# Third group of pair sums moved to the PSUM bank of the first, parts of layer 2 moved two banks on, one gather moved on GpSimd's queue

## The chip, the cores and the metric

The kernel runs on one core of one Trainium2 chip. The metric is the device time of one execution in microseconds (us). TensorE is called PE in the profile, VectorE DVE, ScalarE ACT, GpSimd POOL and SyncE SP. The time of the kernel before is 2491.37 us, the median of 3 runs (2491.12 to 2492.53).

## What is computed

48 embedding tables are looked up for 512 samples, which gives `e` with 48 fields of 32 elements a sample. Three layers of a compressed interaction network follow, each with 128 outputs, and then three dense layers:

```python
def _cin_layer(xi, x0, W, b):
    Wr = W.reshape(Fi, F0, -1)
    out = jnp.einsum('nie,nje,ijo->noe', xi, x0, Wr) + b[None, :, None]
    return jax.nn.relu(out)
x0 = e
xs = [x0]
for W, b in ((W1, b1), (W2, b2), (W3, b3)):
    xs.append(_cin_layer(xs[-1], x0, W, b))
z = jnp.concatenate(xs, axis=1).sum(axis=-1)
h = jnp.concatenate([z, dense_ctx], axis=1)
h = jnp.maximum(h @ W_top1 + b_top1, 0.0)
h = jnp.maximum(h @ W_top2 + b_top2, 0.0)
y = h @ W_top3
```

## The kernel before

**Tiles.** A tile is 128 samples at one of the 32 elements, so there are 4 blocks of 32, 128 tiles in all. Each goes through three layers, and the engines work as a software pipeline: step `v` does the pair sums of layer 1 for tile `v+3` (t0), the products of layer 1 for tile `v+2` (t1), layer 2 for `v+1` (t2) and layer 3 for `v` (t3). In the code `l` is 0 for what leads from layer 1 to layer 2 and 1 for what leads from layer 2 to layer 3. Each of the five engines has its own list of instructions, written out by hand, and they meet at semaphores alone.

**Layer 1** uses that its input is symmetric: products of two fields come out of squares of sums. The fields of the tile, split in a high and a low half-precision part, stand in `x0hl`; a transposing DMA issued by SP (`transpose_x0`, L263) brings them to `x0T`; `pair_sums` (L439) multiplies them with a 0/1 matrix in three groups of 4, 4 and 2 matmuls of 128 columns (groups 0, 1 and 2, ahead of banks 12, 14 and 17 of the step); `square_pairs` on ACT (L589 to L594) squares each group out of PSUM, twice; `stacked_lo` on DVE (L757) makes the low part of the last group, `squares_lo` on POOL (L356) that of the others; and `layer1` (L456) multiplies them with the weights in 28 matmuls of 128 columns, spread over banks 1 to 5 of the next step, into `misc[0]`.

**Layers 2 and 3** have 12 banks each a tile (bank numbers 0 to 11 of a step are layer 2, 12 to 23 layer 3). PE fills a PSUM bank with 3 matmuls of 512 columns (L466), in a ring of 5 banks. ACT and DVE take turns in emptying them, with 4 instructions a bank: ACT writes scaled products (L564), DVE adds into two chains (`fma`, L778). POOL adds up ACT's products (`sum_rest` L332, `sum_all` L345 to L351), helped by one adding DMA of 512 KB a layer and tile, `work<-work` (`add_by_dma`, L325).

**From one layer to the next.** DVE merges the parts (L787, L792), ACT takes the relu (L601), DVE works out a scale in four small steps (L807 to L819), ACT writes the high part (`hi_part`, L608) and the scaled columns (L612), DVE the low part (`lo_part`, L824). Behind the low part SP issues two transposing DMAs, `xT<-hi` and `xT<-lo` (L270, L271). The program of SP in a step is `transpose_x(1, t3)`, `transpose_x0(t0)`, `transpose_x(0, t1)`, in this order, each behind waits of its own. In step `v` the high and low part of `l = 1` stand at bank 1 (ACT) and bank 3 (DVE), those of `l = 0` at banks 8 and 9. DVE's instructions of a bank come only once PE has filled this bank.

**POOL's queue** in a step: `sum_all(1, t3-1)`, `add_by_dma(0, t2)`, every second step `x0_scaled`, two gathers (indirect DMAs, L293, in 24 of the steps of each of the first three blocks), every second step `x0_lo`, then `sum_rest(0)`, `sum_all(0)`, `add_by_dma(1, t3)`, `squares_lo`, and `sum_rest(1)`.

Of the kernel before, what the change touches and what calls it, by code (L numbers as in the profile page):

```python
# [33 lines left out]
P = 128  # L34
# [29 lines left out]
KF = KT - 1  # L64
L1_PASSES = 3 * KF + 1
SETUP = W1_SETUP + 2 * BANKS
PAIR_BANK = (1, 0, 0)
PAIRS_AT = (12, 14, 17)
LAST_USER = [max(m for m in range(BANKS) if (BANKS + m) % RING == r) for r in range(RING)]
SCALE = 4  # L70
# [8 lines left out]
def build(nc, ids, tables, ctx_in, select, pairs_of, w_pair, w_pair_t, w2, w3, b_cin, wt1, bt1, wt2, bt2, wt3, out):  # L79
# [3 lines left out]
    with ExitStack() as stack:  # L83
# [9 lines left out]
        def wait(eng, s, value):  # L93

            if not (isinstance(value, int) and value <= 0):
                eng.wait_ge(s, value)  # L96
# [15 lines left out]
        wst, zst = w1h[:, KF, :], sb("zst", [P, P], f16)  # L112
# [51 lines left out]
        misc = [ps(f"m{n}", [P, Q * P]) for n in range(2)]  # L164
# [23 lines left out]
        s_zt, s_zts = sem("pair_sums_in_psum"), sem("squares_saved")  # L188
        s_zst, s_zl = sem("stacked_squares_ready"), sem("squares_lo")
# [38 lines left out]
        def active(tile):  # L228

            return not isinstance(tile, int) or 0 <= tile < TILES  # L230
# [59 lines left out]
        def _(pool):  # L290
            def gather(b, fields, landed=None):
                for f in fields:
                    pool.indirect_dma_start(  # L293
                        emb[:, b, f, :], None, tables[f],
                        bass.IndirectOffsetOnAxis(ap=ids_sb[:, b, f:f + 1], axis=0)).then_inc(landed or s_gather[b], 16)
# [57 lines left out]
            def squares_lo(t):  # L353

                wait(pool, s_zts, t * 3 + 3)
                pool.tensor_tensor(zl[:], zT[:, 0:KF, :], zh[:], ALU.subtract).then_inc(s_zl, 1)  # L356
# [12 lines left out]
            def step(v, parity, b=None, fields=(), columns=None):  # L369

                t0, t2, t3 = v + 3, v + 1, v
                if active(t3 - 1):
                    sum_all(1, t3 - 1)
                if active(t2):
                    add_by_dma(0, t2)
                if parity == 0 and active(v + 4):
                    x0_scaled(v + 4)
                gather(b, fields)
                if parity == 0 and active(v + 4):
                    x0_lo(v + 4)  # L380
                if active(t2):
                    sum_rest(0, t2)
                    sum_all(0, t2)
                if active(t3):
                    add_by_dma(1, t3)
                if active(t0):
                    squares_lo(t0)
                if columns:
                    spread(b, *columns)
                if active(t3):  # L390
                    sum_rest(1, t3)
# [19 lines left out]
        def _(pe):  # L411
# [17 lines left out]
            def pair_sums(t, g):  # L429

                if g == 0:
                    wait(pe, s_x0t, (t + 1) * 16)
                    wait(pe, s_zts, (t - 1) * 3 + 1)
                elif g == 1:
                    wait(pe, s_pool[0], t + 1)
                else:
                    wait(pe, s_zts, t * 3 + 2)
                for k in range(4 * g, min(4 * g + 4, KT)):
                    ins = nc.tensor.matmul(misc[PAIR_BANK[g]][:, (k % 4) * P:(k % 4 + 1) * P],  # L439
                                           sel[:, k * P:(k + 1) * P], x0T[0:2 * F, :], start=True, stop=True)  # L440
                ins.then_inc(s_zt, 1)
# [4 lines left out]
            def layer1(t, c):  # L446

                if c == 0:
                    wait(pe, s_zts, t * 3 + 3)
                    wait(pe, s_zst, t + 1)  # L450
                for i in range(L1_PASSES * c // 5, L1_PASSES * (c + 1) // 5):
                    if i == 2 * KF + 1:
                        wait(pe, s_zl, t + 1)
                    z, w, k = l1_passes[i]
                    z, w = (z[0:STACK, :], w[0:STACK, :]) if k is None else (z[:, k, :], w[:, k, :])
                    ins = nc.tensor.matmul(misc[0][:, 0:P], z, w, start=i == 0, stop=i == L1_PASSES - 1)  # L456
                if c == 4:
                    ins.then_inc(s_l1, 1)
# [81 lines left out]
        def _(act):  # L540

            act.wait_ge(s_wchain, 16)
            for l in range(2):
                nc.scalar.activation(whi[l][:], raw[l], ACT.Copy, scale=winv[:, 0:1]).then_inc(s_split, 1)
                for n in range(BANKS):
                    i = l * BANKS + n
# [34 lines left out]
            def square_pairs(t, g):  # L581
# [5 lines left out]
                if g == 2:  # L587
                    rest = misc[PAIR_BANK[g]][0:STACK, n * P:(n + 1) * P]
                    nc.scalar.activation(zst[0:STACK, :], rest, ACT.Square, scale=SQUARE)  # L589
# [25 lines left out]
            def step(v, parity):  # L615
                t0, t1, t2, t3 = v + 3, v + 2, v + 1, v
                other = 1 - parity
                for n in range(2 * BANKS):
                    if n in A_BANKS[0] and active(t2):
                        products(0, t2, n, other)  # L620
                    if n - BANKS in A_BANKS[1] and active(t3):
                        products(1, t3, n - BANKS, parity)
                    if n == 4 and active(t1):
                        relu(0, t1)
                    if n == 6 and parity == 1 and active(v + 3):
                        x0_unit(v + 3)
                    if n == 10 and parity == 0 and active(v + 4):
                        x0_hi(v + 4)
                    if n == 8 and active(t1):
                        hi_part(0, t1)  # L630
                        columns(0, t1, parity)
                    if n in PAIRS_AT and active(t0):
                        square_pairs(t0, PAIRS_AT.index(n))
                    if n == 22 and active(t2):
                        relu(1, t2)
                    if n == 1 and active(t3):
                        hi_part(1, t3)
                        columns(1, t3, parity)

            steps(act, step)  # L640


# [17 lines left out]
        def _(dve):  # L660
# [48 lines left out]
            rows = slice(COPIES[2], COPIES[2] + REST)  # L709
# [3 lines left out]
            for i in range(2 * BANKS):  # L713
                l, n = i // BANKS, i % BANKS
# [37 lines left out]
            def stacked_lo(t):  # L752


                rows = slice(COPIES[1], COPIES[1] + REST)
                wait(dve, s_zts, t * 3 + 3)
                nc.vector.tensor_tensor(zst[rows, :], misc[0][rows, 2 * P:3 * P], zst[rows, :],  # L757
                                        ALU.subtract).then_inc(s_zst, 1)

            def fma(layer, t, q, parity):  # L760
# [75 lines left out]
            def step(v, parity):  # L836
                t1, t2, t3 = v + 2, v + 1, v
                other = 1 - parity
                if isinstance(v, int) and v == TILES - 1:
                    x0_over_e(NB - 1)  # L840
                for n in range(2 * BANKS):
                    layer, m = n // BANKS, n % BANKS
                    if m not in D_BANKS[layer]:
                        continue
                    for k in range(Q):
                        if active((t2, t3)[layer]):
                            fma(layer, (t2, t3)[layer], D_BANKS[layer].index(m) * Q + k, (other, parity)[layer])
                        if n == 1 and parity == 0 and active(v + 4):
                            x0_scale(v + 4, k)
                        if n == 3 and active(t3):  # L850
                            if k == 0:
                                lo_part(1, t3)
                            if k == 1:
                                over_e(1, t3)
                        if n == 3 and k == 3 and active(t1):
                            pre1(t1, parity)
                        if n == 7 and active(t1):
                            scale(0, t1, k)
                        if n == 9 and k % 2 == 0 and active(t3 - 1):
                            merge(1, t3 - 1, k // 2)  # L860
                        if n == 9 and active(t1):
                            if k == 1:
                                lo_part(0, t1)
                            if k == 3:
                                over_e(0, t1)
                        if n == 11 and k == 0 and active(t3 - 1):
                            over_e(2, t3 - 1)
                        if n == 20 and k % 2 == 1 and active(t2):
                            merge(0, t2, k // 2)
                        if n == 22 and k == 0 and active(t1 + 1):  # L870
                            stacked_lo(t1 + 1)
                        if n == 23 and active(t2):
                            scale(1, t2, k)
                    if n == 14 and isinstance(v, int) and TILES - NB <= v < TILES - 1:
                        x0_over_e(v - TILES + NB)
# [71 lines left out]
```

## Time and profile before

| | |
|---|---|
| median of 3 runs | 2491.37 us (2491.12 to 2492.53) |
| the profiled execution's own time | 2490.32 us |
| its span, first to last instruction | 2488.5 us |
| mean granted TensorE clock | 0.995 |
| PE busy | 2357.0 us, 95% |
| DVE busy | 2263.7 us, 91% |
| ACT busy | 2143.9 us, 86% |
| POOL busy | 1902.3 us, 76% |

A row of the timeline has the start in us, the duration in us, the engine ("SPq" is SP's queue, where a DMA is issued), the line, the operation, output<-input, the form, and the number of merged instructions; in brackets stand the idle time of the engine before it and what ended this. The ends of matmuls are modelled and overlap, so what PE loses is read from starts. "issue" says that the profile shows nothing that the engine waited for.

### The profile page before, as it was taken

Reading aid. Unit: us, or ns where it says so; the run is one execution under the profiler, and the core shown is the slowest. Engines: PE = TensorE matmul, PEld = TensorE weight load, DVE = VectorE, ACT = ScalarE, POOL = GpSimd, SP = SyncE. Lnnn points to the kernel's source line nnn. Section 1 sums busy time; section 2 is a strip of 40 time slices with the busy share of each in tenths; the row PEclk is TensorE's granted clock in tenths of the full one; section 3 lists DMA queues with packets and bytes.
Section 4 is the critical chain, followed back from the end, with each engine's and each line's share of the span. In section 5 each row is a group of like instructions: output and inputs, shape, how many; then the busy total and the mean of one; then the engine's idle time right before and its main releaser. Section 6 shows DMA issues by size and latency. Waiting matters only on the chain.

```text
span 2488.5 us, 68764 instructions
## 1 busy us (share of the span) xinstructions
PE 2357.0 (95%) x14174; PEld 1163.9 (47%) x14174; DVE 2263.7 (91%) x9404; ACT 2143.9 (86%) x7910; POOL 1902.3 (76%) x1878
## 2 busy tenths in 40 slices
PE   1699999999999999999999999999999999999998
PEld 0344444444544444444444444444454444545443
DVE  6499999999999999999999999999999999999994
ACT  4588989889888898998898989889889899898884
POOL 7388888887778888887778888888777777777762
PEclk9899999999999999999999999999999999999999
DMA  5133333333333333333333333333333333333331
GB/s 167 25 70 68 64 69 71 64 66 69 67 69 62 69 71 69 65 67 68 69 61 69 71 69 66 65 69 70 60 68 69 67 69 61 68 68 68 69 65 32
DMA packets 150316, 168.61 MB, mean 68 GB/s; under 512 B 111956, under 2 KB 115671, under 8 KB 150264
## 3 DMA queue, kind: packets, MB, share of 16 engines
q0 software_dynamic: 43008, 137.39, 29.8%
q1 hardware_dynamic: 107256, 30.73, 5.5%
q14 instruction: 44, 0.36, 0.1%
q8 instruction: 8, 0.13, 0.0%
HBM read 12.82 MB, written 0.00 MB: 5 GB/s over the span
## 4 chain that ended last, share of the span: by engine, by line
PE 57%; ACT 18%; issue 10%; DVE 6%; DMA 3%; POOL 2%; SPq 2%; ACTq 1%; DVEq 1%; POOLq 0%
PE y L466 46%; ACT work L564 10%; PE m L456 6%; PE m L439 4%; ACT work L594 3%; ACT zh L592 3%; DVE acc L778 3%; DMA work<-work 2%; DMA x0T<-x0hl 1%; POOL part L345 1%; ACTq L96 1%; SPq L271 1%; SPq L270 1%; DVEq L96 1%; DVE m L798 0%
## 5 line engine op out<-in xcount | busy, mean ns | idle before, releaser
L466 PE MATMUL y<-whi,xT 128*128 128x512 f16 x6144 | 2006.6, 380 | 19.6 <-DMA xT<-lo 9.4
L778 DVE SCALAR_TENSOR_TENSOR acc<-y,xc,acc 128x128 f32<-128x128 f32 x5632 | 1680.1, 341 | 103.9 <-PE y L466 95.6
L564 ACT ACTIVATE work<-y,xc 128x128 f32<-128x128 f32 x5632 | 1604.5, 389 | 115.8 <-PE y L466 105.3
L466 PE MATMUL y<-wlo,xT 128*128 128x512 f16 x3072 | 1166.2, 380 | 0.0
L466 PEld LDWEIGHTS y<-whi,xT 128*128 128x128 f16 x6144 | 599.9, 98 | 652.0 <-issue 43.9
L345 POOL TENSOR_TENSOR part<-part,work 128x512 f32<-128x512 f32 x384 | 487.0, 1268 | 82.8 <-DMA work<-work 53.1
L466 PEld LDWEIGHTS y<-wlo,xT 128*128 128x128 f16 x3072 | 301.3, 98 | 235.7 <-issue 1.1
L356 POOL TENSOR_TENSOR zl<-work,zh 128x1152 f16<-128x1152 f32 x128 | 347.6, 2716 | 9.3 <-ACT work L594 9.3
L325 POOL DMA_DIRECT2D work<-work x256 | 232.1, 907 | 112.5 <-ACT work L564 111.7
L345 POOL TENSOR_TENSOR part<-work 128x512 f32<-128x512 f32 x128 | 162.7, 1271 | 175.2 <-DMA work<-work 161.0
L293 POOL DMA_INDIRECT emb<-tbl,ids_sb x192 | 197.1, 1027 | 54.1 <-issue 51.3
L439 PE MATMUL m<-x0T,sel 96*128 96x128 f16 x1280 | 137.4, 222 | 84.0 <-DMA x0T<-x0hl 49.5
L592 ACT ACTIVATE zh<-m 128x512 f16<-128x512 f32 (+1 forms) x384 | 201.1, 524 | 7.4 <-PE m L439 3.7
L594 ACT ACTIVATE work<-m 128x512 f32<-128x512 f32 (+1 forms) x384 | 203.2, 529 | 0.0
L348 POOL TENSOR_TENSOR part<-part 128x256 f32<-128x256 f32 x256 | 185.9, 726 | 20.1
L332 POOL TENSOR_TENSOR part<-work 128x512 f32<-128x512 f32 x128 | 163.3, 1276 | 49.5 <-ACT work L564 48.9
L439 PEld LDWEIGHTS m<-x0T,sel 96*128 96x128 f16 x1280 | 83.6, 98 | 232.7 <-issue 106.0
L778 DVE SCALAR_TENSOR_TENSOR ends<-y,xc,acc 128x128 f32<-128x128 f32 x512 | 162.9, 345 | 0.0
L608 ACT ACTIVATE hi<-ends,sc 128x128 f16<-128x128 f32 x128 | 47.0, 367 | 110.3 <-DVE mpw L819 110.3
L351 POOL TENSOR_TENSOR psum<-part 128x128 f32<-128x128 f32 x256 | 116.3, 454 | 20.1
L456 PE MATMUL m<-w1l,zh 128*128 128x128 f16 x1152 | 127.7, 220 | 0.0
L456 PEld LDWEIGHTS m<-w1l,zh 128*128 128x128 f16 x1152 | 92.0, 99 | 60.4 <-issue 1.0
(102 smaller groups left out, 1826.1 us busy)
## 6 DMA issues: line engine op xcount, KB each, us to landing
work<-work POOLq DMA_DIRECT2D x256, 512.0 KB, 4.7
xT<-hi SPq DMA_TRANSPOSE x256, 2.9
xT<-lo SPq DMA_TRANSPOSE x256, 2.4
emb<-tbl,ids_sb POOLq DMA_INDIRECT x192, 3.6
xx<-w SPq DMA_DIRECT2D x4, 768.0 KB, 6.4
work<-w SPq DMA_DIRECT2D x4, 768.0 KB
x0T<-x0hl SPq DMA_TRANSPOSE x128
wt_sb<-W_top SPq DMA_DIRECT2D x1, 768.0 KB
```

Source lines behind the costliest of these rows:

```text
L293: pool.indirect_dma_start(emb[:, b, f, :], None, tables[f], bass.IndirectOffsetOnAxis(ap=ids_sb[:, b, f:f + 1], axis=0)).then_inc(landed o ...
L325: pool.dma_start(p[:, 0:ADDED, :], p[:, ADDED:2 * ADDED, :], accum_op=ALU.add).then_inc(s_dma[layer], 16)
L345: pool.tensor_tensor(a[:], rest, p[:, m, :], ALU.add).then_inc(s, 1)
L348: pool.tensor_tensor(a[:, 0:2 * P], a[:, 0:2 * P], a[:, 2 * P:4 * P], ALU.add).then_inc(s, 1)
L356: pool.tensor_tensor(zl[:], zT[:, 0:KF, :], zh[:], ALU.subtract).then_inc(s_zl, 1)
L439: ins = nc.tensor.matmul(misc[PAIR_BANK[g]][:, (k % 4) * P:(k % 4 + 1) * P], sel[:, k * P:(k + 1) * P], x0T[0:2 * F, :], start=True, stop= ...
L456: ins = nc.tensor.matmul(misc[0][:, 0:P], z, w, start=i == 0, stop=i == L1_PASSES - 1)
L466: ins = nc.tensor.matmul(dst[:], xT[layer][:, parity, a, :], w[layer][:, cols], start=i == 0, stop=i == 2)
L564: nc.scalar.activation(prods[layer][:, a, k * P:(k + 1) * P], bank[:, k * P:(k + 1) * P], ACT.Copy, scale=xc[layer][:, parity, j:j + 1]).t ...
L592: nc.scalar.activation(zh[:, 4 * g:4 * g + n, :].rearrange("p t c -> p (t c)"), misc[PAIR_BANK[g]][:, 0:n * P], ACT.Square, scale=SQUARE)
L594: nc.scalar.activation(zT[:, 4 * g:4 * g + n, :].rearrange("p t c -> p (t c)"), misc[PAIR_BANK[g]][:, 0:n * P], ACT.Square, scale=SQUARE). ...
L778: ins = nc.vector.scalar_tensor_tensor(dst, y, col, mine, ALU.mult, ALU.add)
```

## The change

The third group of pair sums goes to `misc[1]`, where it waits for the squares of group 0 instead of group 1; group 0 of the next tile waits for the last low part that reads this bank (`s_zst`). In `layer1` the wait for the stacked squares moves from the first pass to pass 18 of 28. For `l = 1`, the high part and the columns go from bank 1 to bank 3 on ACT, the low part and the sum over elements (`over_e`) from bank 3 to bank 5 on DVE. On POOL the second of the two gathers goes behind `squares_lo`.

```diff
-PAIR_BANK = (1, 0, 0)
+PAIR_BANK = (1, 0, 1)
...
-                gather(b, fields)
+                gather(b, fields[0:1])
                 if parity == 0 and active(v + 4):
                     x0_lo(v + 4)
...
                 if active(t0):
                     squares_lo(t0)
+                gather(b, fields[1:2])
...
                 if g == 0:
                     wait(pe, s_x0t, (t + 1) * 16)
-                    wait(pe, s_zts, (t - 1) * 3 + 1)
+                    wait(pe, s_zst, t)
                 elif g == 1:
                     wait(pe, s_pool[0], t + 1)
                 else:
-                    wait(pe, s_zts, t * 3 + 2)
+                    wait(pe, s_zts, t * 3 + 1)
...
                 if c == 0:
                     wait(pe, s_zts, t * 3 + 3)
-                    wait(pe, s_zst, t + 1)
                 for i in range(L1_PASSES * c // 5, L1_PASSES * (c + 1) // 5):
+                    if i == 2 * KF:
+                        wait(pe, s_zst, t + 1)
                     if i == 2 * KF + 1:
                         wait(pe, s_zl, t + 1)
...
-                    if n == 1 and active(t3):
+                    if n == 3 and active(t3):
                         hi_part(1, t3)
                         columns(1, t3, parity)
...
-                nc.vector.tensor_tensor(zst[rows, :], misc[0][rows, 2 * P:3 * P], zst[rows, :],
+                nc.vector.tensor_tensor(zst[rows, :], misc[PAIR_BANK[2]][rows, 2 * P:3 * P], zst[rows, :],
                                         ALU.subtract).then_inc(s_zst, 1)
...
-                        if n == 3 and active(t3):
+                        if n == 5 and active(t3):
                             if k == 0:
                                 lo_part(1, t3)
                             if k == 1:
                                 over_e(1, t3)
```

## Rows read from the trace of the kernel before

**Rows 1.** The page's first part: busy time, share of the span, instructions

```profile
PE 2357.0 (95%) x14174; PEld 1163.9 (47%) x14174; DVE 2263.7 (91%) x9404; ACT 2143.9 (86%) x7910; POOL 1902.3 (76%) x1878
```

**Rows 2.** Waits, 200 to 2400 us: who waited for whom, us in total, times, longest

```profile
POOL part L345 <- DMA work<-work: 189.3, 159, 2.4
...
PEld m L439 <- ACT work L594: 82.9, 119, 0.9
...
PEld m L456 <- DVE zst L757: 17.5, 59, 0.4
```

**Rows 3.** Timeline of PE around the pair sums of two tiles

```profile
1480.37 0.40 PE L439 MATMUL m<-x0T,sel 96*128 96x128 f16 x4
...
1483.85 0.38 PE L466 MATMUL y<-whi,xT 128*128 128x512 f16 x1
1484.59 0.29 PE L439 MATMUL m<-x0T,sel 96*128 96x128 f16 x2 [0.36 <-ACT work L594]
...
1498.42 0.38 PE L466 MATMUL y<-wlo,xT 128*128 128x512 f16 x1
1498.63 0.38 PE L466 MATMUL y<-whi,xT 128*128 128x512 f16 x1
1499.02 0.39 PE L439 MATMUL m<-x0T,sel 96*128 96x128 f16 x4
...
1503.00 0.29 PE L439 MATMUL m<-x0T,sel 96*128 96x128 f16 x2
...
1517.16 0.39 PE L439 MATMUL m<-x0T,sel 96*128 96x128 f16 x4
```

**Rows 4.** Line L439, 200 to 2400 us: count, duration, first and last start

```profile
L439 PE MATMUL m<-x0T,sel x1198: 217/219/230, 210.4 to 2398.9; 96*128 96x128 f16 x200
```

**Rows 5.** Timeline of SP's queue, the issues of x0T for the same two tiles

```profile
1496.60 1.18 SPq L263 DMA_TRANSPOSE x0T<-x0hl  x1
...
1514.74 1.18 SPq L263 DMA_TRANSPOSE x0T<-x0hl  x1
```

**Rows 6.** Timeline of DVE: low part, bank 5, bank 7, bank 5 of the next step

```profile
1493.76 0.34 DVE L824 SCALAR_TENSOR_TENSOR lo<-ends,sc,hi 128x128 f16<-128x128 f32 x1
...
1495.25 1.13 DVE L778 SCALAR_TENSOR_TENSOR acc<-y,xc,acc 128x128 f32<-128x128 f32 x4
1496.55 0.35 DVE L778 SCALAR_TENSOR_TENSOR acc<-y,xc,acc 128x128 f32<-128x128 f32 x1 [0.17 <-PE y L466]
...
1513.40 1.13 DVE L778 SCALAR_TENSOR_TENSOR acc<-y,xc,acc 128x128 f32<-128x128 f32 x4
```

**Rows 7.** Timeline of POOL: the wait behind squares_lo, the adding DMAs of layer 2

```profile
1493.47 1.27 POOL L345 TENSOR_TENSOR part<-work 128x512 f32<-128x512 f32 x1 [1.37 <-DMA work<-work]
...
1497.37 0.89 POOL L325 DMA_DIRECT2D work<-work  x1
...
1515.76 0.89 POOL L325 DMA_DIRECT2D work<-work  x1
```

**Rows 8.** Transposes behind an adding DMA: timelines, DMA issues 1166:1170, line L270 200:2400

```profile
1166.76 0.90 POOL L325 DMA_DIRECT2D work<-work  x1 [1.16 <-ACT work L564]
...
1167.38 1.11 SPq L270 DMA_TRANSPOSE xT<-hi  x1
...
xT<-hi SPq DMA_TRANSPOSE x1, 4.6
...
DMA to landing us min/median/max: 2.2/2.9/4.8
```

**Rows 9.** Timeline, a tile whose low part came late: DVE, then PE

```profile
1182.22 0.34 DVE L824 SCALAR_TENSOR_TENSOR lo<-ends,sc,hi 128x128 f16<-128x128 f32 x1
...
1187.46 0.39 PE L439 MATMUL m<-x0T,sel 96*128 96x128 f16 x4 [1.01 <-DMA x0T<-x0hl]
```

**Rows 10.** Head: timeline of PE; then stretches, their PEclk the last but two

```profile
82.61 0.40 PE L439 MATMUL m<-x0T,sel 96*128 96x128 f16 x4 [2.20 <-DVE pooled L831]
...
83.60:90.30 6.70, 4.74 (x21) 2.49 (x22) 1.24 (x5) 2.64 (x10) 2.37 (x1) 0.50 0.08 17
```

## The prediction, made before the changed kernel ran

> **What bounds the kernel now.** I read the busy shares first: PE 95%, the others 76 to 91% [rows 1]. So PE's starts set the time, and what it loses between them is what a change can win. A tile takes 18.38 us: line L439 has 1198 matmuls between 210.4 and 2398.9 us [rows 4], ten a tile, which is 119 periods and the 1.5 us from group 0 to group 1. Next the waits [rows 2]: PE's weight loads wait for ACT's squares (L594), 82.9 us, once a tile. Then PE's timeline [rows 3], by starts. A 512-column matmul follows another after 0.216 us (1498.42 to 1498.63). Group 2 came 3.98 us behind group 0 in one tile (1499.02 to 1503.00) and 4.22 in the other, where 8 pair matmuls (0.44) and 15 bank matmuls (3.24) make 3.68: it lost 0.30 and 0.54, **0.4 a tile**. Group 0 itself lost 0.17 (1498.63 + 0.22 = 1498.85, and it started at 1499.02).
>
> What releases group 0 is the step on which this forecast rests. The page calls this idle time "issue", it shows no landing for x0T. But SP issued x0T at 1496.60 and 1514.74 [rows 5], and group 0 started at 1499.02 and 1517.16 [rows 3]: 2.42 us later both times, to the hundredth. A tile whose low part came late shows it too [rows 9]: the low part started at 1182.22, PE had 1.01 us of idle time put down to x0T, and group 0 started 5.24 us behind the low part. In the ordinary tile that is 1493.76 [rows 6] to 1499.02, 5.26 us. So group 0 already stands at the end of this chain: low part of `l = 1` on DVE, SP's issue of hi, lo and x0T (2.84 us from the low part's start to x0T's issue), landing (2.42). It has a margin of none.
>
> **The change, part by part.**
>
> *Group 2 in the other bank.* Its wait for the squares of group 1 goes. The squares of group 0, for which it waits now, are one product group and one group of squares earlier on ACT, over 2 us. The gain is 0.30 to 0.54 us a tile, I take 0.4. The new wait of group 0 for `s_zst` is for DVE's bank 22 of the step before, half a step earlier: nothing. Moving the `s_zst` wait from pass 0 to pass 18 saves at most the 17.5 us of weight-load waits, 0.15 a tile, and these are mostly hidden beside a running matmul; I take nothing.
>
> *The gather on POOL.* Two gathers stood ahead of the sums, now one; the other goes behind `squares_lo`, where POOL idles 1.37 us for the landing of the adding DMA [rows 7]; over the stretch it is 189.3 us in 159 waits [rows 2]. A gather takes about 1 us and fits. POOL issues the same number of DMAs, and the adding DMA of layer 2 is bound as before, by that landing and the sums behind it. Cost nothing; if the cover were gone, 72 steps x 1 us x the share that reaches PE, some tens of us at most.
>
> *High part and columns from bank 1 to bank 3 on ACT.* ACT waited there for DVE's scale and now fills this with a product group. The low part comes later still, so nothing waits for the high part. Nothing.
>
> *Low part from bank 3 to bank 5 on DVE.* Now the low part starts at 1493.76. Bank 5 on DVE waits for PE to fill it. Bank 7 started after a wait for PE at 1496.55; bank 5 is 6 matmuls, 1.30 us, earlier, so it was ready at 1495.25, which is just when DVE started it [rows 6]. With two instructions fewer ahead of bank 5, DVE will be there early and wait. I call this moment R. The low part now starts at R - 1.49; after the change at R + 0.26 (one instruction of bank 5; 4 take 1.13, each 0.26 behind the other). **It comes 1.75 us later, and with it hi, lo and x0T in SP's queue.** On an idle DMA queue group 0 starts at R + 0.26 + 5.26 = R + 5.52, while PE would be free for it at R + 3.60 (1498.85 - 1495.25). From group 0 to the next R: 1499.02 to 1513.40 is 14.38, without the loss of group 2 **14.08**. The period is a closed loop: 14.08 + 5.52 = 19.60, against 18.38 now, although the gain of group 2 is in it.
>
> *What x0T meets.* The adding DMA of layer 2 is issued at 1497.37 and 1515.76 [rows 7], R + 2.12 and R + 2.36. Now x0T is issued 0.77 and 1.02 us **before** it. After the change x0T is issued at R + 3.10, 0.7 to 1.0 us **behind** it. The adding DMA doesn't slip along: it hangs on ACT's bank 6 and on POOL's sums, which follow from group 0 and PE's banks. What a transpose costs there is shown by an earlier tile [rows 8]: adding DMA at 1166.76, transpose xT<-hi issued 0.62 later, landed 4.6 us after its issue instead of 2.2. That is 5.2 us behind the adding DMA's issue, so it was served only when that was through. The bounds for x0T: 2.4 us (as now) and 4.8 (the longest landing of the line). The nearest row is the one at 0.62; with 0.86 it gives 5.2 - 0.86 = 4.4 us, and 0.1 from landing to the start as for the others. Group 0 then starts at R + 3.10 + 4.5 = **R + 7.6**, the period is 14.08 + 7.6 = **21.7**, +3.3 us.
>
> The Trainium skill says otherwise (DMA: Bandwidth & Descriptors, "Queues, rings and completion order"): each DMA engine takes turns between the queues that have work, packet by packet. By it x0T would be served beside the adding DMA, near 2.4 us. The tile above speaks against it [rows 8]; it is the first rival below.
>
> *PE's clock.* PE would stand idle 4.0 us in each tile (7.6 - 3.6). In the steady stretch no idle time was near this; the long one is 1.01 [rows 9]. In the head, behind idle times of which one was 2.20 at 82.61, the granted clock was 0.50 from 83.6 to 90.3 us [rows 10], that is 1.2 GHz in place of 2.4. So I expect it to fall behind many of the new gaps. Bounds: nothing, and 6.7 us at half speed, 3.35 lost a tile. The head's stretch had more gaps in it, here none follows, so I take half of it, 1.7 us, behind three gaps in four: **1.3 a tile**.
>
> The Trainium skill (TensorE: Matmul & The Clock Gate, "HAM oscillation — how this bites in real kernels") tells of a kernel that waits for a DMA in every tile and starts each one at the low clock. By this the price would be the 1.7 in every tile.
>
> **The sum.** The chain acts in steps 0 to 124, where a low part and an x0T both stand: 124 periods. 124 x (21.7 - 18.38) = 412; 124 x 1.3 = 161; the last three steps lose well under 1 us each. The profiled execution took 2490.32 us (span 2488.5 and 1.8 around it), 1 us under the median of 2491.37, so the sum is the same against either: 2491 + 412 + 161 = **3064 us**.
>
> **The rivals.**
>
> 1. *Queues take turns*, or the adding DMA slips behind x0T: the landing stays at 2.4. 124 x (19.60 - 18.38) = 151: 2642 us, clock unhurt since the idle time is 1.9. For it: x0T has never been issued behind an adding DMA in this trace. Against it: the earlier tile [rows 8], and the two moments lie 0.7 to 1.0 us on the wrong side of each other. The Trainium skill's rule cited above leads here.
> 2. *Collision, but the clock holds*: 2491 + 412 = 2903. For it: the falls in the trace are all in the head, where PE had little work on either side of the gaps.
> 3. *Not slower: group 0 isn't released by x0T.* Its place is the 0.17 us before group 0, which the profile puts down to "issue". If x0T landed early and something else took these 2.42 us, there would be room, and the 0.4 of group 2 would be won: 2491 - 124 x 0.4 = 2441. It decides where x0T lands at R + 3.6 or before. For it only the label; against it the equal 2.42 in both tiles and the late tile [rows 9].
>
> **Chances.** Collision with the clock falling 0.60, without 0.20, rival 1 0.13, rival 3 0.04, the rest spread (above all a collision that costs still more). A measurement of this kernel tells a change from none at about 0.2%, 5 us. Slower by more 0.96, within 0.01, faster 0.03. The range takes in the collision with and without the clock: from 2903 with 0.3 us a tile off for a milder queue, 2860, to 3230, which is 2.6 us of clock a tile. Rival 1 lies outside.
>
> **What would show it.** Right: the 0.4 us ahead of group 2 are gone; the low part starts 0.26 us behind DVE's first instruction of bank 5; x0T is issued 0.7 to 1.0 us behind an adding DMA, and group 0 starts 4.5 us later, about R + 7.6; PE is idle some 4 us ahead of each group 0 and its share falls from 95% to about 80; the granted clock is 0.5 in part of the slices; SP's x0T is still the third of its three. Wrong: a period of 19.6 (rival 1), 21.7 with the clock at 1.0 (rival 2), or group 0 without idle time ahead of it, which would take the whole chain away.

## The result and the profile after

The changed kernel takes **3121.4 us** (median of 6 runs, 3119.43 to 3128.18) against 2491.26 us (6 runs, 2489.04 to 2492.53): a ratio of **1.254**, 95% interval 1.252 to 1.2553. It is a quarter slower. The forecast was 3064, with a range of 2860 to 3230. The times are medians of runs in the chip's usual state; one run of the first experiment, 3093 us at a mean granted clock of 0.746, was not in it and is left out.

The page of the kernel after: busy shares, PE's slices and clock, the chain that ended last, and the group of line L440, which was L439 before.

```profile
PE 2532.4 (81%) x14174; PEld 1254.8 (40%) x14174; DVE 2299.0 (74%) x9404; ACT 2172.6 (70%) x7910; POOL 1900.4 (61%) x1878
...
PEclk6899989999988899889998999899999999899899
...
PE 63%; DMA 19%; SPq 10%; DVE 3%; issue 3%; POOL 2%; DVEq 0%; ACT 0%; ACTq 0%; POOLq 0%
...
L440 PE MATMUL m<-x0T,sel 96*128 96x128 f16 x1280 | 171.2, 264 | 542.6 <-DMA x0T<-x0hl 537.9
```

PE did the same 14174 matmuls, but is busy for 81% in place of 95% [rows 1]. The chain that ended last has 19% on DMA and 10% on SP's queue. PE's idle time ahead of the pair sums is 542.6 us, and nearly all of it ended with the landing of x0T.

Waits of the kernel after, 200 to 3000 us, the three with the largest totals, in us, times and longest:

```profile
POOL work L325 <- ACT work L566: 553.8, 122, 7.2
PEld m L440 <- DMA x0T<-x0hl: 530.3, 119, 5.5
PE m L440 <- DMA x0T<-x0hl: 471.8, 119, 5.1
```

The wait of the pair sums for ACT's squares [rows 2] is gone from the list. In its place PE waits once a tile for x0T, 4.0 us each (471.8 in 119).

One tile without gathers, on DVE, SP, POOL and PE (timeline of the kernel after; the first row is the first instruction of bank 5 on DVE):

```profile
1551.92 0.35 DVE L780 SCALAR_TENSOR_TENSOR acc<-y,xc,acc 128x128 f32<-128x128 f32 x1 [0.38 <-PE y L468]
1552.19 0.34 DVE L826 SCALAR_TENSOR_TENSOR lo<-ends,sc,hi 128x128 f16<-128x128 f32 x1
...
1552.56 1.09 SPq L270 DMA_TRANSPOSE xT<-hi  x1
1553.70 1.23 SPq L271 DMA_TRANSPOSE xT<-lo  x1
1555.03 1.88 SPq L263 DMA_TRANSPOSE x0T<-x0hl  x1
...
1554.24 0.87 POOL L325 DMA_DIRECT2D work<-work  x1
...
1559.30 0.40 PE L440 MATMUL m<-x0T,sel 96*128 96x128 f16 x4 [3.62 <-DMA x0T<-x0hl]
```

DVE waits for PE ahead of bank 5, so R is 1551.92. The low part starts 0.27 us later, x0T is issued at R + 3.11, 0.79 us behind the adding DMA (R + 2.32), and group 0 starts at R + 7.38, 4.27 us behind the issue where it was 2.42 [rows 3, 5].

What the DMA queues moved in this tile, first from 1555.60 to 1558.25 us, then from 1558.25 to 1559.05 (q0 is POOL's queue, q1 SP's; number of packets, MB, share of 16 engines):

```profile
q0 software_dynamic: 128, 0.52, 109.6%
q1 hardware_dynamic: 28, 0.00, 0.5%
...
q1 hardware_dynamic: 288, 0.07, 41.4%
q0 software_dynamic: 16, 0.00, 2.7%
```

In the first stretch the adding DMA starts its 128 packets of 4096 bytes. SP's queue has only 28 packets of 4 bytes there, none with data. The packets with the data of x0T (128 of 256 bytes) are all in the second stretch: none of them ran beside the adding DMA's data.

Line L263 and line L440 of the kernel after, 200 to 3000 us: issue times, landing, and the matmuls' count and starts:

```profile
L263 SPq DMA_TRANSPOSE x0T<-x0hl x120: 1164/1799/2062, 206.4 to 2998.1; - x120
...
DMA to landing us min/median/max: 4.1/4.6/5.6
...
L440 PE MATMUL m<-x0T,sel x1190: 216/230/315, 211.1 to 2984.7; 96*128 96x128 f16 x199
```

Every x0T landed 4.1 us or more behind its issue, not one as before. 119 tiles lie between 211.1 and 2984.7, less the 5 us or so from group 0 to group 2 of the last one: 118 periods of 23.5 us, against 18.38 [rows 4]. By tile, x0T landed after a median of 4.2 us in the 47 tiles without gathers and of 4.7 in the 67 with two.

The clock, over the steady stretch and two single tiles (PEclk is the last column but two):

```profile
200.00:3000.00 2800.00, 2326.16 (x13136) 1153.67 (x13133) 2098.31 (x8724) 1995.39 (x7346) 1732.90 (x1706) 0.92 0.29 53
1489.40:1513.70 24.30, 20.68 (x110) 10.09 (x110) 17.39 (x71) 17.00 (x63) 15.33 (x16) 0.85 0.26 49
1537.83:1559.30 21.47, 17.85 (x111) 9.08 (x111) 17.39 (x71) 16.74 (x63) 15.31 (x16) 1.00 0.31 57
```

The tile from 1537.83 to 1559.30 ran at the full clock and took 21.47 us. The one from 1489.4 took 24.3 us at a mean of 0.85, with the same work on PE (one matmul at its edge apart). The mean of the stretch is 0.92, so a sixth of the time was at the lower level of 1.2 GHz. In 104 of the 119 tiles the clock fell for a part (means from 0.85 to 0.98); 15 ran at 1.00 throughout.

### The profile page after: what moved, and what is told of

Its sections match the earlier page's. It is cut to its first block, busy times and chain, and to the rows that moved or that the text cites. A ratio compares the mean times of both kernels' runs of the same rounds, so it can differ in the third digit from the quotient of the medians.

```text
span 3119.6 us, 68697 instructions
## 1 busy us (share of the span) xinstructions
PE 2532.4 (81%) x14174; PEld 1254.8 (40%) x14174; DVE 2299.0 (74%) x9404; ACT 2172.6 (70%) x7910; POOL 1900.4 (61%) x1878
## 4 chain that ended last, share of the span: by engine, by line
PE 63%; DMA 19%; SPq 10%; DVE 3%; issue 3%; POOL 2%; DVEq 0%; ACT 0%; ACTq 0%; POOLq 0%
PE y L468 52%; DMA x0T<-x0hl 18%; PE m L458 6%; SPq L271 5%; SPq L270 5%; PE m L440 4%; POOL emb L293 1%; DVE lo L826 1%; DVE acc L780 1%; DMA xT<-lo 0%; DVEq L96 0%; DMA work<-work 0%; PE m L523 0%; PE y L530 0%; PE y L523 0%
## 5 line engine op out<-in xcount | busy, mean ns | idle before, releaser
L468 PE MATMUL y<-whi,xT 128*128 128x512 f16 x6144 | 2127.6, 403 | 17.5 <-DMA xT<-lo 16.3
L566 ACT ACTIVATE work<-y,xc 128x128 f32<-128x128 f32 x5632 | 1588.2, 377 | 435.2 <-PE y L468 424.9
L468 PE MATMUL y<-wlo,xT 128*128 128x512 f16 x3072 | 1238.2, 403 | 0.0
L468 PEld LDWEIGHTS y<-whi,xT 128*128 128x128 f16 x6144 | 631.5, 103 | 704.4 <-issue 146.8
L440 PE MATMUL m<-x0T,sel 96*128 96x128 f16 x1280 | 171.2, 264 | 542.6 <-DMA x0T<-x0hl 537.9
L440 PEld LDWEIGHTS m<-x0T,sel 96*128 96x128 f16 x1280 | 120.2, 120 | 696.5 <-DMA x0T<-x0hl 556.9
L774 DVE SCALAR_TENSOR_TENSOR acc<-y,xc,bcin 128x128 f32<-128x128 f32 x256 | 89.3, 349 | 399.8 <-PE y L468 392.0
L367 POOL TENSOR_TENSOR x0hl<-xs,x0hl 128x96 f16<-128x96 f32 x64 | 23.4, 366 | 238.6 <-ACT x0hl L572 238.6
L572 ACT ACTIVATE x0hl<-xs 128x96 f16<-128x96 f32 x64 | 18.1, 283 | 199.4 <-DMA x0T<-x0hl 186.1
```

The source lines that it names most:

```text
L468: ins = nc.tensor.matmul(dst[:], xT[layer][:, parity, a, :], w[layer][:, cols], start=i == 0, stop=i == 2)
L566: nc.scalar.activation(prods[layer][:, a, k * P:(k + 1) * P], bank[:, k * P:(k + 1) * P], ACT.Copy, scale=xc[layer][:, parity, j:j + 1]).t ...
```

## The experiments

Two theories were set against others. First, that all of the loss is the closed loop low part, SP's queue, x0T, group 0, and that it has two parts, 1.75 us of delay and the stay behind the adding DMA. Second, that the clock adds to it because PE stands idle for 4 us.

### The low part back at its place

```diff
-                    if n == 3 and active(t3):
+                    if n == 1 and active(t3):
                         hi_part(1, t3)
...
-                        if n == 5 and active(t3):
+                        if n == 3 and active(t3):
                             if k == 0:
                                 lo_part(1, t3)
```

> The changed kernel with the high and low part of layer 2 back at banks 1 and 3; bank of the third group, the moved wait and the moved gather stay. Theory (the move of the low part makes the whole loss, the other edits gain a little): x0T lands as before, 0.3 to 0.5 us a tile ahead of group 2 are won, 2491 - 50 = about 2441 us, and the granted clock is 1.0. Rival (the bank or the gather carries part of the loss): over 2491 us. Rival (the 0.4 us only move to group 0, since x0T's transpose follows at the end of the chain at DVE): 2480 to 2491.

Measured: **2443.2 us** beside 2491.9, ratio 0.9804 (0.9791 to 0.9818). The whole loss of 630 us hangs on this one move, and what is left of the change is a gain of 49 us (47 in the repetition below, whose profile is the one used).

### The move alone

```diff
-                    if n == 1 and active(t3):
+                    if n == 3 and active(t3):
                         hi_part(1, t3)
...
-                        if n == 3 and active(t3):
+                        if n == 5 and active(t3):
                             if k == 0:
                                 lo_part(1, t3)
```

> The kernel before with only the high and low part of layer 2 moved two banks on. Theory: the closed loop through the low part is all of it, so the loss is all here: 3121 us and 0 to 50 more, because the wait of group 2 for the squares of group 1 stays in the loop. Rival (the loss needs the bank or the gather too): clearly under 3100 us.

Measured: **3128.1 us**, ratio 1.2563 (1.2543 to 1.2582), 7 us over the changed kernel, which the two intervals don't tell from nothing. So bank and gather are worth some 48 us without the move and about 7 with it. The traces show two reasons. PE's wait for ACT's squares at group 2 is shorter here, 23.7 us over 200 to 3000 us against 82.9 in the kernel before, and DVE's merge no longer waits for POOL's sum. And what is left is partly hidden by the clock: in tiles at full clock and without gathers the period is 21.76 us here (13 tiles) against 21.50 in the changed kernel (12 tiles), but the clock fell less here, to a mean of 0.92 in place of 0.91 over the run. Why it fell less is open.

### x0T ahead of the other transposes

```diff
-                if active(t3):
-                    transpose_x(1, t3, parity)
                 if active(t0):
                     transpose_x0(t0, 1 - parity)
+                if active(t3):
+                    transpose_x(1, t3, parity)
```

> The changed kernel with one swap on SP: x0T is issued ahead of the two transposes of layer 2, so its landing no longer hangs on the low part. Theory: group 0 is free; bank 12 then waits for xT<-lo, issued 1.77 us behind R and landing 2.4 later, R + 4.2 against R + 3.8 where PE would start it: 0.4 us a tile lost, 0.4 won at group 2, so 2450 to 2500 us at a clock of 1.0. Rival (the completion of xT<-lo is held up by the adding DMA as well, whose issue is 0.5 us behind it): bank 12 starts near R + 7, some 2.9 us a tile lost, over 2800 us. Rival (x0T isn't what releases group 0): stays at 3121 us.

Measured: **2479.3 us**, ratio 0.9944 (0.9929 to 0.9959). The low part is as late as in the changed kernel, and 642 of its us are gone by moving one issue of SP ahead of two others. Timeline of this kernel, one tile on SP and then PE:

```profile
1510.32 1.10 SPq L263 DMA_TRANSPOSE x0T<-x0hl  x1
1520.99 1.09 SPq L270 DMA_TRANSPOSE xT<-hi  x1
1522.13 1.23 SPq L271 DMA_TRANSPOSE xT<-lo  x1
...
1524.54 0.39 PE L468 MATMUL y<-whi,xT 128*128 128x512 f16 x1 [0.20 <-DMA xT<-lo]
```

x0T goes out over 10 us ahead of xT<-hi, not behind it. Bank 12 now waits for xT<-lo, 2.41 us behind its issue, and PE loses a few tenths of a us there, as the theory had it. In most tiles the completion of xT<-lo isn't held up: of 92 waits for it the median ends 2.43 us behind the issue, with the adding DMA of layer 2 issued a median of 0.58 us behind xT<-lo. Where it is issued only 0.3 us behind, bank 12 starts up to 3.9 us behind the issue, as at 2032.18.

### The adding DMA made small

```diff
+                n = 16 if layer == 0 else Q * P
-                pool.dma_start(p[:, 0:ADDED, :], p[:, ADDED:2 * ADDED, :], accum_op=ALU.add).then_inc(s_dma[layer], 16)
+                pool.dma_start(p[:, 0:ADDED, 0:n], p[:, ADDED:2 * ADDED, 0:n], accum_op=ALU.add).then_inc(s_dma[layer], 16)
```

> The changed kernel, but the adding DMA of layer 2 moves 16 of each 512 columns: the rest of this addition is left out, so the sums of layer 2 lack these terms. Theory (x0T stands behind the bytes of the adding DMA): x0T lands 2.4 us after its issue, group 0 at R + 5.5, a period of 19.6 us without clock falls, 124 x 1.2 over 2491, about 2640 us. Rival (the late landing comes from the issue or from the queue itself and not from the bytes): x0T still lands over 4 us after its issue and the time is near 3100 us. Rival (the clock falls at idle times of 1.9 us too): 2640 plus over 100 us.

Measured: **2647.4 us**, ratio 1.0629 (1.0613 to 1.0645), where the loop without a collision gave 2642. Timeline of this kernel, POOL, SP and PE:

```profile
1511.00 1.25 POOL L326 DMA_DIRECT2D work<-work  x1
...
1511.69 1.18 SPq L263 DMA_TRANSPOSE x0T<-x0hl  x1
...
1514.13 0.40 PE L441 MATMUL m<-x0T,sel 96*128 96x128 f16 x4 [1.78 <-DMA x0T<-x0hl]
```

x0T is still issued 0.69 us behind the adding DMA, but group 0 starts 2.44 us behind its own issue. The queues in the 0.6 us from 1512.8 to 1513.4:

```profile
q0 software_dynamic: 246, 0.02, 81.3%
q1 hardware_dynamic: 112, 0.03, 36.8%
```

The adding DMA has more packets here than with all its columns, 246 of them in this stretch alone, but of 64 bytes, and the packets of x0T run among them. So it is the bytes of the other transfer that hold x0T, not its issue and not the number of its packets. Delay alone costs 156 us; at idle times of 1.8 us the clock hardly falls (0.981 over the run, 1.00 from 200 to 2400 us).

### PE kept busy while it waits

```diff
+FILL = 12
...
+                    wait(pe, s_zst, t)
+                    for _ in range(FILL):
+                        nc.tensor.matmul(misc[1][:], w1h[:, 0, :], whi[0][:, 0:Q * P], start=True, stop=True)
                     wait(pe, s_x0t, (t + 1) * 16)
-                    wait(pe, s_zst, t)
```

> The changed kernel with 12 more matmuls of 512 columns on PE ahead of each group 0, into the free bank, before PE waits for x0T; nothing reads them. They take 2.6 of the about 4 us that PE idles there. Theory (the granted clock falls because of this idle time, and costs some 200 us of the loss): the clock stays near 1.0, the periods are those of the tiles of the changed kernel whose clock didn't fall, 21.5 us without and 22.0 us with gathers, so 2491 + 124 x 3.4 = about 2915 us: added work makes it faster. Rival (the clock costs nothing, since the loop runs through DVE and the DMA): 3121 us. Rival (added work is paid): 3121 + 124 x 2.6 = 3440 us.

Measured: **2926.2 us**, ratio 1.1741 (1.1723 to 1.1759): 1536 matmuls more, and 195 us faster than the changed kernel. Timeline of PE, then the clock of the steady stretch:

```profile
1499.56 2.75 PE L436 MATMUL m<-whi,w1h 128*128 128x512 f16 x12
1503.41 0.40 PE L443 MATMUL m<-x0T,sel 96*128 96x128 f16 x4 [1.10 <-DMA x0T<-x0hl]
...
200.00:2800.00 2600.00, 2434.04 (x14458) 1219.30 (x14457) 2076.37 (x8650) 1963.99 (x7293) 1723.53 (x1693) 1.00 0.31 56
```

The idle time is down to 1.1 us (median of all tiles 1.4), the granted clock is 1.00 in place of 0.92. The clock's share of the loss is thus 195 us, 1.6 us a tile, the rest of the loop 435. The changed kernel's own tiles say the same: its 15 tiles at full clock have a median period of 21.5 us without gathers and 22.0 with two, the tiles here 21.5 and 21.9.

### Half the way

```diff
-                            if k == 0:
+                            if k == 2:
                                 lo_part(1, t3)
-                            if k == 1:
+                            if k == 3:
                                 over_e(1, t3)
```

(in bank 3, on the kernel of the first experiment)

> The kernel of e1_low_back with the low part and the sum over elements of layer 2 two instructions of bank 3 later on DVE (behind its third and fourth instruction, not its first and second): 0.52 us later, and x0T is still issued ahead of the adding DMA. Theory (no slack at group 0, each 0.1 us of delay of the low part is 0.1 us a tile): 2443 + 124 x 0.35 to 0.52 = 2486 to 2508 us. Rival (there was slack, only the step past the adding DMA costs): 2443 to 2455 us. Rival (already here x0T falls behind the adding DMA in some tiles): over 2550 us.

Measured: **2559.0 us** (2549.94 to 2580.65), ratio 1.0264 (1.0243 to 1.0286): the third of the cases, the collision begins already here. Timeline of this kernel, two tiles, SP, POOL and PE:

```profile
1135.60 1.16 SPq L263 DMA_TRANSPOSE x0T<-x0hl  x1
1136.19 0.90 POOL L325 DMA_DIRECT2D work<-work  x1
1137.92 0.40 PE L440 MATMUL m<-x0T,sel 96*128 96x128 f16 x4 [0.29 <-DMA x0T<-x0hl]
...
1154.19 1.18 SPq L263 DMA_TRANSPOSE x0T<-x0hl  x1
1154.41 0.91 POOL L325 DMA_DIRECT2D work<-work  x1
1158.08 0.40 PE L440 MATMUL m<-x0T,sel 96*128 96x128 f16 x4 [2.31 <-DMA x0T<-x0hl]
```

In the first tile x0T was issued 0.59 us ahead of the adding DMA and group 0 started 2.32 us behind it. In the second it was 0.22 us ahead and 3.89. Between them there is no jump but a slope. Over the 120 tiles of this trace group 0 starts 2.3 us behind the issue where x0T was 0.54 us or more ahead, mostly 3.1 at 0.46 to 0.49, 3.6 to 3.9 at 0.2 to 0.25, and 5.1 below 0.1. The queues in the second tile, from 1155.25 to 1155.75 us and then to 1157.75, show what is held up:

```profile
q1 hardware_dynamic: 128, 0.03, 29.6%
...
q0 software_dynamic: 96, 0.39, 104.1%
q1 hardware_dynamic: 32, 0.00, 2.2%
```

All 128 data packets of x0T start before the first one of the adding DMA. But the 32 packets of 4 bytes that end the transposing DMA come among the adding DMA's 96 of 4096 bytes, and group 0 waits for this end. In the first tile they came ahead of them.

0.52 us of delay cost 116 us over the first experiment, about twice what the delay alone would (43 to 64). A part of this is the clock: it fell in 17 of the 120 tiles of the profiled execution (which took 2580.65 us, the longest of the five), nearly always behind idle times of 1.9 us or more, to a mean of 0.91 in most.

### Bank alone, gather alone

The kernel before with only one of the two other edits. The first has the bank and its waits (in part shown; the wait moved to pass 18 and the bank that `stacked_lo` reads are in it too):

```diff
-PAIR_BANK = (1, 0, 0)
+PAIR_BANK = (1, 0, 1)
...
-                    wait(pe, s_zts, (t - 1) * 3 + 1)
+                    wait(pe, s_zst, t)
...
-                    wait(pe, s_zts, t * 3 + 2)
+                    wait(pe, s_zts, t * 3 + 1)
```

> The kernel before with only the bank of the third group and its waits changed (e1_low_back without the move of the gather). Theory (the gather is hidden where it stood and where it goes): 2443 us within 5, the same as e1_low_back. Rival (the gather behind squares_lo is worth something, POOL's sums come 1.3 us earlier in 72 steps): 5 to 30 us slower than e1_low_back.

Measured: **2468.6 us**, ratio 0.9905 (0.989 to 0.992). The rival held: 25 us slower than with the gather moved too.

The second has the gather:

```diff
-                gather(b, fields)
+                gather(b, fields[0:1])
...
                     squares_lo(t0)
+                gather(b, fields[1:2])
```

> The kernel before with only the second gather moved behind squares_lo. Theory (the gather moves POOL's sum ahead of DVE's merge, which in the kernel before waits for it 17.2 us in all, and 45.4 once group 2 is faster): 5 to 17 us faster, 2474 to 2486 us. Rival (additive, worth the same 25 us as beside the bank): 2466 us. Rival (PE waits for ACT at group 2 anyway, nothing to win): 2491 us.

Measured: **2474.3 us**, ratio 0.9927 (0.9913 to 0.994), 18 us faster than before, at the edge of the theory's 2474 to 2486. DVE's merge waits for POOL's sum for 2.3 us over 200 to 2400 us, where it waited 17.2. Alone the two are worth 23 and 18 us, together some 48. The kernel of the first experiment again:

> The kernel of e1_low_back once more, for a profile of it to be read beside that of e7_bank_alone. Theory: 2443 us again. In the trace the waits of DVE's merge of layer 2 for POOL's sum (45.4 us in the steady stretch of e7_bank_alone) are mostly gone, since the sums start one gather earlier, and x0T is issued over 0.9 us ahead of the adding DMA in nearly all tiles. Rival (the 25 us between the two kernels came from another place): these waits stay near 45 us.

Measured: 2445.4 us, ratio 0.9812 (0.9797 to 0.9827). The waits of DVE's merge for POOL's sum, 200 to 2400 us, first with the bank alone, then with the gather moved too:

```profile
DVE msum L788 <- POOL psum L351: 45.4, 60, 1.5
...
PE y L467 <- DVE acc L779: 30.1, 44, 1.2
```

```profile
DVE msum L789 <- POOL psum L351: 19.6, 51, 1.3
...
PE y L468 <- DVE acc L780: 5.8, 12, 1.0
```

Both fell by some 25 us: with two gathers ahead of them POOL's sums were late for DVE, DVE was late for the bank, and PE waited for it.

### The best of it

The first experiment with the swap on SP:

```diff
-                if active(t3):
-                    transpose_x(1, t3, parity)
                 if active(t0):
                     transpose_x0(t0, 1 - parity)
+                if active(t3):
+                    transpose_x(1, t3, parity)
```

> e1_low_back with x0T issued first on SP. Theory (group 0 still waits 0.2 to 0.3 us a tile for x0T there): this goes too, bank 12 has its operands 1.3 us ahead, PE's own work of 17.7 us a tile is nearly all that is left: 2405 to 2435 us, faster than both kernels. Rival (DVE or ACT takes over as what PE waits for): 2436 to 2445 us.

Measured: **2436.2 us**, ratio 0.9782 (0.9769 to 0.9795), the lowest time of this study, though just outside the theory's 2405 to 2435: the rival's case. Its interval touches those of the first experiment (0.9791 to 0.9818) and its repetition, so the 7 us between them are at the edge of what can be told. Waits of it, 200 to 2400 us:

```profile
DVE msum L789 <- POOL psum L351: 46.7, 93, 2.4
...
PE y L468 <- DVE acc L780: 20.9, 59, 1.3
```

No wait of group 0 for x0T is left in its list, but DVE's wait for POOL and PE's for DVE are back, 46.7 and 20.9 us. The 0.15 to 0.2 us a tile won at group 0 went for the most part to the next waits of the ring.

## Why the prediction was right, and where it was off

**The releaser of group 0.** Right. It rested on two equal distances of 2.42 us where the page said "issue"; over the 120 tiles from 200 to 2400 us the trace of the kernel before has 2.40 to 2.43 us in 113. The swap on SP (2479 us) and the undone move (2443) show it from both sides.

**The delay of the low part.** Right in each term: PE from group 0 to R 14.09 us (1537.83 to 1551.92; forecast 14.08), low part at R + 0.27 (0.26), x0T at R + 3.11 (3.10). By itself it costs 156 us, shown with the small adding DMA (forecast 151).

**The collision.** Right in mechanism and nearly in size. In the tile above group 0 stood at R + 7.38 (7.6), a period of 21.47 (21.7). Over all tiles the term came out a little larger, since landings had a median of 4.6 us, up to 5.6, and not the 4.4 taken: with the clock held up, the whole is 2926 - 2491 = 435 us, where the forecast had 412. The longer landings are those of the tiles with gathers, 4.7 us against 4.2 in the median; by which way the gathers lengthen them is not shown. The rule that the queues take turns packet by packet (the Trainium skill, DMA: Bandwidth & Descriptors, "Queues, rings and completion order") gave, as the forecast read it, 2642 us, which is what came out only when the other transfer was made small; with its 512 KB in place each x0T landed 4.1 us or more behind its issue. The forecast was right to leave this rival, but it had read more into the rule than that section says. The section counts some 9 to 17 descriptors as one packet, and an engine goes to another queue only between packets. The profile has 144 rows for the adding DMA (128 of 4096 bytes and 16 of 4), which is nine for each of the 16 engines if they are spread evenly. If these nine are one packet, the rule itself lets x0T wait for all of them, as measured. What the runs refute is a change of turns after each 4096 bytes. Where a packet ended no run shows.

**The clock.** Right that it falls, the term was mis-sized: 1.3 us a tile forecast, 161 us, and 1.6 us measured, 195 us. The Trainium skill (TensorE: Matmul & The Clock Gate, "HAM oscillation — how this bites in real kernels") has it fall in every tile of such a kernel. Here 104 of 119 tiles had it, where I took three in four; the one from 1537.83 ran at 1.00 throughout, behind 4.0 us from start to start of PE's matmuls, as long as in many tiles whose clock fell. What decides it between these tiles the runs don't show. With 1.7 us in every tile, 211 us, that page was nearer than I was. The sign I gave, slices of the page at 0.5, didn't come: a slice is 78 us, and their means are 0.8 and 0.9 behind the head.

**Group 2.** The 0.4 us a tile were to be 50 us. Measured alone the bank is worth 23 us: behind it stood POOL's late sums, so that only with the gather moved 48 came out. Alone this term is half of what I took. In the changed kernel the wait itself is gone as forecast: group 2 came 3.70 us behind group 0 (1537.83 to 1541.53; forecast 3.68). What this wins there is some 0.26 us in a tile at full clock, measured beside the move alone, where I took 0.30; the time shows only 7 us of it.

**The gather, at nothing.** This step was wrong: it is worth 18 us alone and 25 beside the bank. I named the idle time behind `squares_lo` that takes the gather in, and did not ask what came earlier on POOL's queue because of it. The merge's wait for POOL was in the list of waits of the kernel before, 32.7 us over the run, and I read past it. It changed next to nothing in the sum, since x0T's loop hides it there (7 us between the move alone and the whole change, for bank and gather together).

Two terms were thus too small, by 23 us (the loop: 5 of them the delay, 18 the collision) and by 34 us (clock). That makes the 57 us between 3064 and 3121.

## What to carry to other kernels

An issue order on a DMA queue is a dependency: what stands behind a late operand is late with it, though it needs nothing of it, and issuing x0T ahead of two transposes that it doesn't need was worth 642 us here. Ask of each step moved back which DMA is issued behind it, how much margin its reader has, and which large transfer it slides past; 0.37 us nearer to it cost 1.57 us in a tile. And when an edit moves work to an idle place, look at what follows the place that it left.

## What was not expected

- A transpose issued 0.22 us **ahead** of the 512 KB adding DMA was held up too, 3.89 us to group 0 in place of 2.32. I had taken the order of the issues for the edge; it lies about 0.5 us ahead. Its data had moved, and its last small packets had not. The first experiment and the kernel before stand just clear of this edge: their x0T is issued 0.56 us ahead at the least.
- 1536 matmuls that nobody reads, 12 in each wait, made the kernel 195 us faster, by holding the granted clock at 1.00 in place of 0.92.
- SP's issue of x0T itself took longer behind the adding DMA, 1.88 us in place of 1.18 [rows 5], and pushed the two transposes behind it back by 0.7 us. PE waited for neither from 200 to 3000 us.
